# Row maxima of attention scores turned by one transpose instead of four, in a transformer layer on one core

## The reference

```python
x = x + attn(layernorm(x))        # q, k, v = x @ W.T + b, split into 16 heads of 8
scores = einsum('bhqd,bhkd->bhqk', q, k) / sqrt(8);  scores = where(tril, scores, NEG)
out = einsum('bhqk,bhkd->bhqd', softmax(scores), v) @ Wo.T + bo
x = x + ffn(layernorm(x))         # sel = argmax(x @ gate_w.T), rw = sigmoid(max)
# per expert e: xs = x * rw * (sel == e);  out += (xs @ w_up[e].T * silu(xs @ w_gate[e].T)) @ w_down[e].T
```

## Time and profile before

| | |
|---|---|
| median of 3 runs | 568.27 us (565.29 to 571.53) |
| the profiled execution | 567.53 us, span 565.8 us |
| TensorE busy | 534.4 us (94%) |
| VectorE busy | 454.1 us (80%) |
| ScalarE busy | 379.5 us (67%) |
| GpSimd busy | 209.5 us (37%) |
| attention units | from about 70 us to about 413 us |

### The profile page before, as it was taken

One profiled execution on the slowest core, in us unless ns is written; L12 is line 12 of the kernel. 1 busy time (PEld: TensorE's weight loads), 2 busy tenths in 40 slices (PEclk: granted clock), 3 DMA queues, 4 the chain that ended last, 5 costly groups with the idle time before them and its releaser, 6 DMA issues.

```text
span 565.8 us, 12240 instructions
## 1 busy us (share of the span) xinstructions
PE 534.4 (94%) x4658; PEld 235.3 (42%) x4658; DVE 454.1 (80%) x669; ACT 379.5 (67%) x770; POOL 209.5 (37%) x393
## 2 busy tenths in 40 slices
PE   4559999999999999999999999999989999999996
PEld 4325433333343332433434334334224455666653
DVE  8847999999999999999999999999923556555631
ACT  1234588898898989889889899898885422222221
POOL 3677364453353443524544346214232111111100
PEclk9879999999999999999999999999997999999999
DMA  6051121420211512102232021120030122111000
GB/s 172 14 154 56 59 63 35 148 56 16 68 30 42 155 32 63 52 21 69 75 107 67 11 65 45 39 69 8 7 101 2 48 57 61 56 57 54 22 19 20
DMA packets 27867, 32.45 MB, mean 57 GB/s; under 512 B 4385, under 2 KB 21281, under 8 KB 27809
## 3 DMA queue, kind: packets, MB, share of 16 engines
q1 hardware_dynamic: 27664, 31.28, 19.4%
q10 hardware_dynamic: 144, 0.39, 0.2%
HBM read 20.26 MB, written 11.01 MB: 55 GB/s over the span
## 4 chain that ended last, share of the span: by engine, by line
PE 69%; DVE 20%; ACT 4%; issue 2%; POOL 2%; DMA 1%; SPq 1%; POOLq 0%; DVEq 0%
PE ps L1058 19%; PE ps L1042 13%; PE ps L999 8%; DVE top_p L823 7%; DVE top_p L821 7%; PE ps L1111 6%; PE ps L1119 5%; PE ps L1108 5%; DVE top_p L816 3%; ACT prob L676 3%; PE ps L1009 3%; PE ps L1109 2%; PE ps L935 2%; PE ps L944 1%; PE ps L1075 1%
## 5 line engine op out<-in xcount | busy, mean ns | idle before, releaser
L676 ACT ACTIVATE prob<-ps 128x512 f32<-128x512 f32 (+2 forms) x640 | 307.8, 561 | 42.7 <-PE ps L1042 37.7
L823 DVE TENSOR_REDUCE top_p<-ps 128x2 f32<-128x1024 f32 x192 | 223.7, 1218 | 4.8 <-PE ps L999 1.2
L1042 PE MATMUL ps<-q_rows,k_rows 51*128 51x512 bf16 (+3 forms) x768 | 169.0, 328 | 2.7 <-ACT prob L676 1.4
L1058 PE MATMUL ps<-prob,v_all 128*9 128x512 f32 (+3 forms) x1536 | 157.8, 492 | 0.5 <-ACT sum_sb L667 0.4
L580 POOL TENSOR_SCALAR_AFFINE_SELECT prob<-prob 128x512 f32<-128x512 f32 x128 | 81.3, 635 | 184.9 <-ACT prob L676 183.1
L999 PE MATMUL ps<-k_rows,q_rows 48*128 48x512 bf16 (+2 forms) x896 | 130.6, 305 | 7.3 <-DMA k_rows<-split_parts 5.0
L1042 PEld LDWEIGHTS ps<-q_rows,k_rows 51*128 51x128 bf16 x768 | 52.3, 93 | 135.5 <-ACT prob L676 120.3
L821 DVE TENSOR_REDUCE top_p<-ps 128x4 f32<-128x1024 f32 x64 | 76.5, 1215 | 0.9 <-PE ps L1009 0.6
L999 PEld LDWEIGHTS ps<-k_rows,q_rows 48*128 48x128 bf16 x896 | 42.6, 94 | 43.8 <-issue 13.3
L719 ACT ACTIVATE prob<-ps 128x512 f32<-128x512 f32 x32 | 19.1, 597 | 56.0 <-PE ps L1109 56.0
L899 DVE TENSOR_TENSOR prob<-ps,prob 128x512 f32<-128x512 f32 x32 | 22.1, 690 | 38.4 <-PE ps L1111 38.4
(11 more groups left out here) (90 smaller groups left out, 420.5 us busy)
## 6 DMA issues: line engine op xcount, KB each, us to landing
split_parts<-part SPq DMA_DIRECT2D x6, 768.0 KB, 5.8
q_rows<-split_parts SPq DMA_DIRECT2D x31, 96.0 KB
k_rows<-split_parts SPq DMA_DIRECT2D x31, 96.0 KB
value_sums<-sum_sb SPq DMA_DIRECT2D x128, 18.0 KB
x_sb<-x SPq DMA_DIRECT2D x8, 256.0 KB, 4.9
qk<-value_sums SPq DMA_DIRECT2D x8, 256.0 KB, 3.7
qk<-inverse_sums SPq DMA_DIRECT2D x8, 256.0 KB, 3.9
out<-y SPq DMA_DIRECT2D x8, 256.0 KB, 2.3
```

Source lines behind the costliest of these rows:

```text
L676: a.activation(prob[:, i % NB, g0:g0 + heads, 0:cols], ps[:, load_at(u, n) % 3, 0:heads * cols].rearrange("p (s t) -> p s t", s=heads), AC ...
L823: return v.tensor_reduce(top_p[:, place, qt, s:s + 3:2], banks, AX.X, ALU.max)
L1042: last = mm(ps[:, l % 3, m * cols:(m + 1) * cols], k_rows[rows, k, s + m, j * P:(j + 1) * P], q_rows[rows, k, s + m, c * HALF + q0:(c + 1) ...
L1058: last = mm(ps[32 * g:32 * g + HD + 1, BANK_V, q0:HALF], v_all[:, b, j, first_head + g, :], prob[:, i % NB, g, 0:n], start=(j == 0), stop= ...
```

## The change

What a turn moves is laid out anew. `top_part` holds the maxima of a half as 48 columns in the order (group, part, s, tile of 128 queries); one transpose makes 48 rows of 128 of them, VectorE copies 48 x 128, and each of the two DMAs of `send_top` takes 24 rows of 128 (256 bytes a row, where there were 6 rows of 1024 bytes) to the same three rows of `q_rows`. So that these land in one run, `q_rows` and `k_rows` hold half, then head, then token. The DRAM tensor has this order too, and the weights' columns are permuted on the way in (`by_unit`) so that s stands first on the partitions; `send_parts` therefore issues two DMAs, one for each s, where it issued one. What `split_out` is waited for doubles.

```diff
-    split = nc.dram_tensor("split_parts", (2, 3, UNITS, HD, GH * SEQ), BF16, kind="Internal").ap()
+    split = nc.dram_tensor("split_parts", (2, 3, UNITS, HD, 2, 2, GH // 2, HALF), BF16, kind="Internal").ap()
...
-        q_rows = sb("q_rows", [P, 3, 2, SEQ], BF16)
-        k_rows = sb("k_rows", [P, 3, 2, SEQ], BF16)
+        q_rows = sb("q_rows", [P, 3, 2, 2, HALF], BF16)
+        k_rows = sb("k_rows", [P, 3, 2, 2, HALF], BF16)
...
-        top = sb("top", [P, 2, TPH, GH])
-        top_rest = sb("top_rest", [P, 2, TPH, GH])
-        top_part = sb("top_part", [P, 2, TPH, 2, 3, 2], BF16)
-        top_rows = sb("top_rows", [12, 2, HALF], BF16)
+        top = sb("top", [P, 2, GH, TPH])
+        top_rest = sb("top_rest", [P, 2, GH, TPH])
+        top_part = sb("top_part", [P, 2, 2, 3, 2, TPH], BF16)
+        top_rows = sb("top_rows", [TOP_COLS, 2, P], BF16)
...
             def send_parts(b, h, units=range(UPB)):
                 sp.wait_ge(part3_set[h], b + 1)
-                rows = UPB * b + units.start, UPB * b + units.stop
-                sp.dma_start(split[:, :, rows[0]:rows[1], :, :]
-                             .rearrange("s n u d (g t) -> (u d g) (s n) t", g=GH)
-                             [:, :, h * HALF:(h + 1) * HALF],
-                             part[32 * units.start:32 * units.stop, h, :, :, :].rearrange("p s n t -> p (s n) t")
-                             ).then_inc(split_out[h], 16)
+                for s in range(2):
+                    sp.dma_start(split[:, :, UPB * b + units.start:UPB * b + units.stop, :, :, h, s, :]
+                                 .rearrange("e n u d r t -> (u d r) (e n) t"),
+                                 part[64 * s + 16 * units.start:64 * s + 16 * units.stop, h, :, :, :]
+                                 .rearrange("p e n t -> p (e n) t")).then_inc(split_out[h], 16)
...
                 for rg in range(2):
-                    sp.dma_start(q_rows[64 * rg + ROWS:64 * rg + ROWS_M, k, :, c * HALF:(c + 1) * HALF],
-                                 top_rows[6 * rg:6 * rg + 6, c, :]).then_inc(top_in[k][c], 16)
+                    sp.dma_start(q_rows[64 * rg + ROWS:64 * rg + ROWS_M, k, c, :, :],
+                                 top_rows[TOP_COLS // 2 * rg:TOP_COLS // 2 * (rg + 1), c, :]).then_inc(top_in[k][c], 16)
...
             def turn(c, r):
-                src = ps[0:12, pair_banks(r).start, :].bitcast(BF16)[:, 0:HALF]
+                src = ps[0:TOP_COLS, pair_banks(r).start, :].bitcast(BF16)[:, 0:P]
                 return v.tensor_copy(top_rows[:, c, :], src)
...
-                v.tensor_reduce(top[:, c].rearrange("p i g -> p (i g)"),
-                                top_p[:, 0:2 + c, c * TPH:(c + 1) * TPH, :].rearrange("p r i g -> p (i g) r"),
+                v.tensor_reduce(top[:, c].rearrange("p g i -> p i g"),
+                                top_p[:, 0:2 + c, c * TPH:(c + 1) * TPH, :].rearrange("p r i g -> p i g r"),
                                 AX.X, ALU.max).then_inc(top_set, 1)
...
             def turn(c, r):
-                bank_b = ps[0:12, pair_banks(r).start, :].bitcast(BF16)
-                for i in range(TPH):
-                    last = nc.tensor.transpose(bank_b[:, i * P:(i + 1) * P],
-                                               top_part[:, c, i].rearrange("p r n s -> p (r n s)"), ident_b[:])
-                return last
+                bank_b = ps[0:TOP_COLS, pair_banks(r).start, :].bitcast(BF16)
+                return nc.tensor.transpose(bank_b[:, 0:P],
+                                           top_part[:, c].rearrange("p r n s i -> p (r n s i)"), ident_b[:])
```

More of the change, by code:

```diff
@@ L25 @@
 ROWS_M = ROWS + 3
+TOP_COLS = 2 * 3 * 2 * TPH
 INV_COLS = HEADS * SEQ // P
@@ L300, in load_half @@
             k = u % 3
-            heads = slice(2 * rg * SEQ, (2 * rg + 2) * SEQ)
             for first_row, n in PART_ROWS:
@@ L304, in load_half @@
                 rows = slice(64 * rg + first_row * HD, 64 * rg + (first_row + n) * HD)
-                eng.dma_start(q_rows[rows, k, :, :].rearrange("p s t -> p (s t)"),
-                              split[0, q_part, u, :, None, heads].to_broadcast((HD, n, 2 * SEQ))
+                eng.dma_start(q_rows[rows, k, :, :, :].rearrange("p c s t -> p (c s t)"),
+                              split[0, q_part, u, :, rg, None, :, :, :].rearrange("d e c s t -> d e (c s t)")
+                              .to_broadcast((HD, n, 2 * SEQ))).then_inc(rows_in[k], 16)
+                eng.dma_start(k_rows[rows, k, :, :, :].rearrange("p c s t -> p (c s t)"),
+                              split[1, 0:n, u, :, rg, :, :, :].rearrange("n d c s t -> d n (c s t)")
                               ).then_inc(rows_in[k], 16)
-                eng.dma_start(k_rows[rows, k, :, :].rearrange("p s t -> p (s t)"),
-                              split[1, 0:n, u, :, heads].rearrange("n d t -> d n t")).then_inc(rows_in[k], 16)
         FRONT = (4, 7, 8)
@@ L359, in _ @@
             for h in range(2):
-                sp.wait_ge(split_out[h], 16)
+                sp.wait_ge(split_out[h], 32)
             sp.wait_ge(k_rows_set, 1)
@@ L365, in _ @@
             for h in range(2):
-                sp.wait_ge(split_out[h], 32)
+                sp.wait_ge(split_out[h], 64)
             load_rows(1)
@@ L387, in step @@
                         for h in range(2):
-                            sp.wait_ge(split_out[h], 16 * ((u + 2) // UPB + 2))
+                            sp.wait_ge(split_out[h], 32 * ((u + 2) // UPB + 2))
                     load_rows(u + 2)
@@ L517, in take_rest @@
                 pool.wait_ge(qk_set[h], 2 * b + 2)
-                pool.wait_ge(split_out[h], 16 * (b + 1))
+                pool.wait_ge(split_out[h], 32 * (b + 1))
                 chain.link(g.tensor_copy(part[:, h, :, 0, :], qk[:, b % 3, h, :, :]))
@@ L533, in split_top @@
                     pool.wait_ge(use_mm, USE["turn", u - 1, c] + 1)
-                src = top[:, c].rearrange("p i (r s) -> p i r s", r=2)
-                rest_of = top_rest[:, c].rearrange("p i (r s) -> p i r s", r=2)
+                src = top[:, c].rearrange("p (r s) i -> p r s i", r=2)
+                rest_of = top_rest[:, c].rearrange("p (r s) i -> p r s i", r=2)
                 parts = top_part[:, c]
[L537 to L540, removed]
+                chain.link(g.tensor_copy(parts[:, :, 0, :, :], src))
+                chain.link(g.tensor_tensor(rest_of, src, parts[:, :, 0, :, :], ALU.subtract))
+                chain.link(g.tensor_copy(parts[:, :, 1, :, :], rest_of))
+                g.tensor_tensor(parts[:, :, 2, :, :], rest_of, parts[:, :, 1, :, :],
                                 ALU.subtract).then_inc(top_part_set, 1)
@@ L657, in _ @@
             for h in range(2):
-                act.wait_ge(split_out[h], 16)
+                act.wait_ge(split_out[h], 32)
             act.wait_ge(k_rows_set, 1)
@@ L999, in piece @@
                         last = mm(ps[:, first_bank + rg, m * width:(m + 1) * width],
-                                  q_rows[rows, k, s, qt * P:(qt + 1) * P],
-                                  k_rows[rows, k, s, k0:k0 + width],
+                                  q_rows[rows, k, qt // TPH, s, qt % TPH * P:(qt % TPH + 1) * P],
+                                  k_rows[rows, k, k0 // HALF, s, k0 % HALF:k0 % HALF + width],
                                   start=(m == 0), stop=not masked[0], skip_group_check=True)
@@ L1042, in load @@
                     last = mm(ps[:, l % 3, m * cols:(m + 1) * cols],
-                              k_rows[rows, k, s + m, j * P:(j + 1) * P],
-                              q_rows[rows, k, s + m, c * HALF + q0:(c + 1) * HALF],
+                              k_rows[rows, k, j // TPH, s + m, j % TPH * P:(j % TPH + 1) * P],
+                              q_rows[rows, k, c, s + m, q0:HALF],
                               start=True, stop=True)
@@ L1177, in by_unit @@
     def by_unit(w):
-        return np.ascontiguousarray(w.reshape(-1, HEADS // GH, GH, HD).transpose(0, 1, 3, 2)).reshape(-1, DIM)
+        of_head = w.reshape(-1, HEADS // GH, 2, GH // 2, HD)
+        return np.ascontiguousarray(of_head.transpose(0, 3, 1, 4, 2)).reshape(-1, DIM)
     rows = EXPERTS * INNER
```

## The result

| | before | after |
|---|---|---|
| median of 4 runs | 569.9 us (565.29 to 571.98) | 576.14 us (573.16 to 577.27) |
| the profiled execution | 567.53 us, span 565.8 | 576.58 us, span 574.8 |
| TensorE busy | 534.4 us | 537.5 us |
| VectorE busy | 454.1 us | 448.0 us |
| DMA packets, of these under 512 bytes | 27867, 4385 | 29177, 6080 |

The ratio of the times is 1.0111, with a 95% interval of 1.0064 to 1.0157, and the medians lie 6.2 us apart: slower. The forecast was 567.7 us with a range of 562.7 to 570.8, and it is wrong. (Of the 8.4 us between forecast and result, 1.6 are the kernel before itself, whose median a fourth run moved from 568.27 to 569.9.) VectorE does 6.1 us less work and the kernel still takes longer.

The account below looks back on a forecast made before the run. A cycle alternating between VectorE's reductions and TensorE's pieces was taken as the bound, not either engine's busy share. Terms -0.75 (turn 'b'), -0.17 (last unit), +0.35 (opening) gave -0.6 us: 567.7 us, range 562.7 to 570.8.

Parts of the forecast that it names:

- Turns: Both turns of each unit: three fewer transposes and a shorter copy, gaining 0.75 us at 'b' and 0.17 in the last unit.
- the term forecast there: At turn 'b', the piece's matmuls start 0.05 us earlier, 15 units, 0.75 us in all.
- The first rival: TensorE or VectorE is full after all: both turns gain, 563.2 us, or about 562.6 with VectorE as only bound; chance 0.20.
- Small DMAs: Two DMAs of maxima behind a turn's copy: issue time unchanged at 0.7 us, at most 0.2 later landing, zero on the path.
- The room: Behind turn 'a', time between the maxima's landing and the first load needing them: 0.2 to 1.1 us, plus the copy's 0.19.
- A wait of line 1041 for DMA of top_rows: Sign on TensorE's loads that was to prove the rival of small DMAs coming too late.
- this rival: Small DMAs come too late for the first load of a unit's second half: 13 to 27 us slower, 581 to 595; chance 0.06.
- Writes of parts: SyncE's queue: ten issues of 0.39 us become twenty, eight new ones hidden in queue time, only the opening pays, +0.35 us.
- The third rival: Doubled writes on the queue delay more than the opening: ten extra issues on the path, 3.9 us, 571.6 us; chance 0.04.
- Opening: At the kernel's start, the second write issue delays the row loads: +0.35 us, between -0.4 and +0.55.

Follow-up runs that it names:

- The doubled copy: The changed kernel with the writes of parts moved behind the next unit's first maxima, plus VectorE's 48 x 128 copy done twice each turn: 569.75 us in one run.
- the four-DMA experiment: The kernel before with one transpose and a 48 x 128 copy, old layout and writes, four DMAs a turn instead of two: 578.4 us, ratio 1.0158.
- layout alone: The changed kernel with four transposes, 12 x 512 copy and 1024-byte rows back in, keeping new order and doubled writes: 577.55 us, ratio 1.0129.
- writes alone: The kernel before with each write of parts cut into two DMAs of half the partitions, nothing else: 574.46 us, ratio 1.0119.
- the late writes: The changed kernel with writes of parts in units 1, 5 and 9 behind the next unit's first maxima, GpSimd's step one unit later: 570.15 us, ratio 1.0017.

## Why the prediction was wrong

*Turns: right.* The copy at 190 to 230 ns, 0.6 to 0.7 us of idleness behind it, 32 transposes, a period 0.05 us shorter: all as forecast. At 'b' the piece's matmuls start 0.06 us after the reduction's end (154.04 for 153.98), where it was 0.11, which is the term forecast there. TensorE's busy time, forecast to fall by some 5 us, rose by 3.1, which fits the half-clock stretches. The first rival, TensorE or VectorE as a full resource, would have shown a period of 22.4. The doubled copy settles VectorE's side of it by an experiment.

*Small DMAs: right.* Their issue time did not move, and behind 'a' nobody waits for them. The room was put at 0.2 to 1.1 us plus 0.19; by the four-DMA experiment it is about 1.2. The rule of the Trainium skill that was weighed there (DMA: Bandwidth & Descriptors, Specifications: 512 bytes as the least transfer for line rate) does not show in these: the queue takes 728 ns an issue for rows of 256 bytes and 726 for rows of 1024, and no landing came too late behind 'a'. (That no row of the trace before has such a transfer was not quite so: its page counts 4385 packets under 512 bytes.) One sign was chosen badly. "A wait of line 1041 for DMA of top_rows" was to prove this rival; the wait came, three times, and it comes with rows of 1024 bytes as well (layout alone, writes alone). It shows that the maxima are late, not why.

*Writes of parts: wrong, and this is the failed step.* It said that "eight of the ten new ones lie where the queue has time: it waited 131.7 us for the copies of line 827". The place and the price are both wrong in that step. The 131.7 us are a sum over the span, 24 waits of up to 11.6 us, and a sum does not say where. The queue's slack lies behind the maxima; the writes stand ahead of them, in a unit where DMAs for values, the two writes, twelve row loads and four more for values follow each other with hardly a pause. There the queue was already 2.9 us late against the copy, and only about 1.3 us were left until TensorE would notice (a delay of 108.78 to 113.13 in the trace, less the 1.3 by which all of it was later, is 3.05 us; it cost 1.73). The timeline of the queue around the writes, in the trace of the kernel before, would have told it: it starts its maxima at 108.78 while their copy stands at 105.48.

The price decided. 0.39 us is the median of ten issues that stood alone or in twos. Four in a row took 4.62 us at the first place, the last of them 1.7, so the two new issues cost 3.6 us there and not 0.8. With 0.8 us even this place would have held them, inside its 1.3. No row of the kernel before has four writes in a row, but a hint is in its queue: the loads of rows right behind the two writes took 1.14 and 1.39 us to issue, their like some places on 0.65. A bound of 1.75 us an issue, which the prediction took for the small DMAs, would have given 3.5 us for two, far over the room.

The third rival had the right kind of loss, "delay more than the opening", at 3.9 us in all (its 571.6 counts the opening's 0.35 twice) and a chance of 0.04. Its working was another: ten extra issues of 0.39 us, all on the path. With four issues at 4.62 less 0.98 us, in three units, and less 1.3 of room each, it would have been 3 x 2.3 = 7 us, against the 5.2 measured. That sum needs the measured price; the place alone would have given nothing.

*Opening: nearly right, in part by luck.* +0.35 was forecast. The loads of rows start 0.40 us later (32.13 for 31.73), and at 32.10 to 32.14 in the three experiments with the layout alone, the split writes and the late writes. The first piece comes 0.54 us later here, and 0.10, 0.57 and 0.90 later in those three, since the last load of rows takes 3.84 to 4.70 us to land. The forecast had no term for that.

*The median.* The stalls (5.2), the other units (-1.0) and the opening up to the first piece (0.5) make about 4.7 of the 6.2 us. The other 1.5 are within the scatter of the runs; in the profiled pair another 4 go with the clock. Why the half-clock stretches fall as they do is open: the mean granted clock goes from 0.967 to 0.988 over the runs of the kernel before, and the profiles of the layout alone and of the late writes have such stretches in other places. No run here ties them to the change.

## What to carry to other kernels

An edit that makes more DMAs out of one is costed at its place in the queue: look at what stands behind it there, when that was ready, and when it is needed, not at the queue's total idle time. And price the row of issues as it will stand, with the longest issue of the trace as a bound, not with the median of single ones. A queue can be late for its next item without anyone waiting; the slack is then the distance to the consumer, here 1.3 us, and an edit that ignores it can use it up. Before shortening an operation in a ring of two buffers, ask whether its duration or its slot is what is paid: here a copy of half the length, or done twice, moved a unit by 0.05 us.

## What was unexpected of the hardware

- Two writes of 768 KB back to back held the issuing queue for 0.98 us, four of 384 KB for 4.56 to 4.99 us (four kernels, three places each), and a single one up to 1.92. The issue time of a DMA is not a property of the DMA alone: the load of rows behind the four took 1.58 us to issue, its like a few places later 0.65. The bytes are the same, so one reading is that the queue had filled up; no run tests it.
- A DMA that takes 24 rows of 256 bytes issued in 728 ns, one of 6 rows of 1024 in 726.
- A transpose of 48 columns has a latency of 235 ns, one of 12 columns 219 ns: four small ones cost by their number, 0.39 us together.
